# Causal attention with a routed feed-forward: maxima, exponentials, layer-norm steps and transposes in another order

## What is computed

```python
latent_kv = x @ w_kv_down;  kv = latent_kv @ w_kv_up        # keys and values, 16 heads of 64
q = (x @ w_q).reshape(Bx, Tx, N_HEAD, HEAD_SIZE)
att = jnp.einsum('bqhd,bkhd->bhqk', q, k) * scale
att = jax.nn.softmax(jnp.where(causal, att, -jnp.inf), axis=-1)
y = jnp.einsum('bhqk,bkhd->bqhd', att, v).reshape(Bx, Tx, HD) @ w_out
...
expert = jnp.argmax(feats @ centroids.T, axis=1)            # of eight
h = (xs - mu) * rsqrt(var + EPS) * g + b
y = xs + relu(h @ W1e.T + b1e) @ W2e.T + b2e                # the expert's own weights
out = alpha * y + (1.0 - alpha) * feats                     # alpha = sigmoid(feats . centroid)
```

## Time and profile before

| what | value |
|---|---|
| runs shown, median (lowest to highest) | 1460.65 us (1459.31 to 1461.14) |
| the profiled execution, its own time | 1459.58 us |
| its span, first to last instruction | 1457.7 us |
| mean granted TensorE clock, as a share of full speed | 0.977 |
| PE busy | 1343.0 us, 92% |
| DVE busy | 1234.4 us, 85% |
| ACT busy | 1083.2 us, 74% |
| POOL busy | 809.8 us, 56% |

### The profile page before, as it was taken

One profiled execution on the slowest core, in us unless ns is written; L12 is line 12 of the kernel. 1 busy time (PEld: TensorE's weight loads), 2 busy tenths in 40 slices (PEclk: granted clock), 3 DMA queues, 4 the chain that ended last, 5 costly groups with the idle time before them and its releaser, 6 DMA issues.

```text
span 1457.7 us, 34718 instructions
## 1 busy us (share of the span) xinstructions
PE 1343.0 (92%) x9120; PEld 1210.6 (83%) x9120; DVE 1234.4 (85%) x4806; ACT 1083.2 (74%) x3186; POOL 809.8 (56%) x1216
## 2 busy tenths in 40 slices
PE   7999999999999999999999999999999999599993
PEld 6988898888888988888888888888888888488872
DVE  5899888888888888888888888888888887499994
ACT  5888787878787878788787878787878886366661
POOL 3445555555555555555555555555555554178886
PEclk9999999999999999999999999999999999699997
DMA  4000000000000000000000000000000000312120
GB/s 194 5 9 12 12 11 12 11 8 11 12 11 12 11 11 10 9 11 11 11 11 12 11 10 11 10 11 12 11 12 11 9 9 14 95 48 63 59 62 8
DMA packets 38793, 32.39 MB, mean 22 GB/s; under 512 B 4882, under 2 KB 35990, under 8 KB 38304
## 3 DMA queue, kind: packets, MB, share of 16 engines
q1 hardware_dynamic: 31968, 21.61, 4.9%
q0 software_dynamic: 4608, 8.67, 1.7%
q10 hardware_dynamic: 2112, 1.11, 0.3%
HBM read 20.35 MB, written 12.07 MB: 22 GB/s over the span
## 4 chain that ended last, share of the span: by engine, by line
DVE 46%; issue 22%; ACT 18%; POOL 6%; PE 5%; ACTq 1%; DMA 1%; DVEq 1%; POOLq 0%; SPq 0%
DVE nscore L851 15%; DVE p_lo L861 13%; ACT prob L722 10%; ACT t_hi L694 5%; DVE nmax L851 2%; POOL prob L1037 2%; DVE ff L367 2%; DVE hitr L891 2%; DVE wup_s L384 1%; DVE on L393 1%; POOL pay L1056 1%; DVE fn L793 1%; DVE gg L402 1%; DVE t_lo L838 1%; DVE rinv L832 1%
## 5 line engine op out<-in xcount | busy, mean ns | idle before, releaser
L1037 POOL TENSOR_TENSOR prob<-prob,rinv 128x256 f32<-128x256 f32 (+1 forms) x512 | 413.2, 828 | 507.8 <-DVE rinv L832 507.7
L722 ACT ACTIVATE prob<-nscore,nmax 128x128 f32<-128x128 f32 (+1 forms) x1024 | 458.7, 449 | 248.4 <-DVE nmax L851 248.4
L851 DVE CUSTOM_DVE_ANT_0 nscore<-psS,mask 128x128 f32<-128x128 f32 (+1 forms) x1024 | 319.9, 350 | 0.0
L861 DVE TENSOR_TENSOR p_lo<-psP,p_hi 128x768 fp32r<-128x768 f32 x256 | 243.7, 952 | 1.0 <-ACT p_hi L694 0.9
L838 DVE TENSOR_TENSOR t_lo<-psT,t_hi 128x512 fp32r<-128x512 f32 x256 | 175.9, 687 | 56.0 <-ACT t_hi L694 56.0
L607 PE MATMUL psP<-ident,prob 128*128 128x128 f32 x1536 | 216.4, 277 | 6.8 <-DVE p_lo L861 6.7
L694 ACT ACTIVATE p_hi<-psP 128x768 fp32r<-128x768 f32 x256 | 204.9, 800 | 1.6 <-PE psP L607 1.6
L579 PE MATMUL psS<-t_lo,xt_hi 128*128 128x256 f32 (+1 forms) x512 | 196.8, 384 | 0.0
L722 ACT ACTIVATION_READ_ACCUMULATOR prob<-nscore,nmax 128x1 f32 x1024 | 191.3, 187 | 0.0
L607 PEld LDWEIGHTS psP<-ident,prob 128*128 128x128 f32 x1536 | 167.2, 141 | 22.7 <-POOL prob L1037 8.8
L867 DVE TENSOR_TENSOR z_lo<-psZU,z_hi 128x512 fp32r<-128x512 f32 x256 | 175.7, 686 | 3.3 <-ACT z_hi L694 3.3
(11 more groups left out here) (167 smaller groups left out, 3246.0 us busy)
## 6 DMA issues: line engine op xcount, KB each, us to landing
fin<-routed_rows SPq DMA_DIRECT2D x40, 136.0 KB, 2.2
wx<-ffn_w SPq DMA_DIRECT2D x2, 2058.0 KB, 12.0
xin<-x SPq DMA_DIRECT2D x32, 128.0 KB, 2.1
xres<-x SPq DMA_DIRECT2D x32, 128.0 KB, 2.1
out<-res,fin POOLq DMA_INDIRECT x80, 2.3
routed_rows<-padr ACTq DMA_DIRECT2D x4, 272.0 KB, 4.3
routed_rows<-padr SPq DMA_DIRECT2D x4, 272.0 KB, 5.4
wup_s<-wup SPq DMA_DIRECT2D x1, 1024.0 KB, 4.9
```

The costliest lines, as they stand in the source:

```text
L722: last = nc.scalar.activation(prob[:, p1, h, a:z], nscore[:, h, a:z], ACT.Exp, bias=nmax[:, p1, h, q:q + 1], scale=-1.0, accum_out=rsum[:, ...
L851: last = v.tensor_tensor_reduce(nscore[:, h, a:z], psQ[q][:, h, :], mask[:, a:z], -1.0, -MASKED, ALU.add, ALU.min, nmax[:, p1, h, q:q + 1])
L861: v.tensor_tensor(p_lo[:, (s - 3) % 2], psP[:, :, 0:384], p_hi[:, (s - 3) % 2].bitcast(F32), ALU.subtract).then_inc(S["p_split"], 1)
L1037: last = g.tensor_tensor(pr, pr, rinv[:, p2, :, q:q + 1].broadcast_to([P, 2, z - a]), ALU.mult)
```

## The change

Four orders are changed; no instruction is added or removed but one or two that a register needs.

1. PE: once the first few slots are over, P stands behind S, ahead of Z (new function `turn_probs`).
2. ACT: `exps(1)` follows `exps(0)` at once, and `z_hi` comes behind both.
3. DVE: `score_max(1)` stands ahead of `p_lo`. What `misc` did at the top of slots 0 to 3 (`an`, `st3`, `fn`, `st1`, `xn`) is now `block_norms`, between `score_max(1)` and `p_lo`; the aggregation of `st3` and `st1` is `block_moments`, behind `p_lo`. `xt_lo` (r = 6) and `st2` (r = 7) stay at the top. The last step of the routing's argmax, `oh`, now has `score_max(1)` ahead of it.
4. POOL: the two steps that make the reciprocal deviation for `fn` stay in slot 1 with semaphores of their own; the four that make the second one move to slot 2.

```diff
+            def turn_probs(g0, s, live):
+                p3 = (s - 3) % 4
+                pe.wait_ge(S["norm_ready"], g0 + s - 2)
+                if live(4):
+                    pe.wait_ge(S["p_split"], g0 + s - 3)
+                for h in range(2):
+                    for k in range(3):
+                        last = nc.tensor.transpose(psP[:, h, k * P:(k + 1) * P],
+                                                   prob[:, p3, h, k * P:(k + 1) * P], ident[:])
+                last.then_inc(S["pt_ready"], 1)
...
-                if live(3):
...
+                if live(3) and setup_slot(s, live):
+                    turn_probs(g0, s, live)
...
                         scores(q, (s - 1) % 2, xb, 2 * (g0 + s - 2) + 1 + q if live(2) else None)
+                if live(3) and not setup_slot(s, live):
+                    turn_probs(g0, s, live)
...
                 if live(1):
                     exps(0)
+                    exps(1)
...
                     cp(z_hi[:, (s - 4) % 2], psZ[:]).then_inc(S["z_hi_done"], 1)
-                if live(1):
-                    exps(1)
...
                 route(b0, s, live_b, 3)
+                if live(1):
+                    score_max(1)
                 route(b0, s, live_b, 4)
+                block_norms(b0, s, live_b)
                 if live(3):
                     dve.wait_ge(S["p_hi_done"], g0 + s - 2)
                     v.tensor_tensor(p_lo[:, (s - 3) % 2], psP[:, :, 0:384], p_hi[:, (s - 3) % 2].bitcast(F32),
                                     ALU.subtract).then_inc(S["p_split"], 1)
-                if live(1):
-                    score_max(1)
+                block_moments(b0, s, live_b)
...
-                    dve.wait_ge(S["r3_steps"], 6 * n - 4)
+                    dve.wait_ge(S["rs3_done"], n)
```

More of the change, by code:

```diff
@@ L149, in block_kernel @@
             bias_done bias_added weights_ready
-            x_loaded xr_loaded st1_done mv1_done ve1_done rs1_done xn_ready xk_hi_done xn_tr xt_hi_done x_split xk_split
+            x_loaded xr_loaded ve3_done rs3_done st1_done mv1_done ve1_done rs1_done xn_ready xk_hi_done xn_tr xt_hi_done x_split xk_split
             t_ready t_hi_done t_split s_ready nmax_ready probs_ready rinv_ready norm_ready pt_ready p_hi_done p_split
@@ L917, in route, with block_moments @@
                         v.tensor_copy(dst[:, db, :], dstf[:]).then_inc(S["dest_ready"], 1)
-            def misc_stats(b0, s, live_b):
+            def block_moments(b0, s, live_b):
                 r, db = s % PAIRS, s // PAIRS
@@ L925, in misc_stats, with block_norms @@
                     aggregate(st1, mv1, S["st1_done"], S["mv1_done"], b0 + db + 2)
+            def misc_stats(b0, s, live_b):
+                r, db = s % PAIRS, s // PAIRS
                 if r == 7 and live_b(1):
                     aggregate(st2, mv2, S["st2_done"], S["mv2_done"], b0 + db)
-            def misc(g0, b0, s, live, live_b):
+            def block_norms(b0, s, live_b):
                 r, db = s % PAIRS, s // PAIRS
+                n = b0 + db - 1
                 if r == 0 and live_b(2):
-                    n = b0 + db - 1
                     dve.wait_ge(S["rs2_done"], n)
@@ L962, in misc @@
                     prep_norm((db + 1) % 2, b0 + db + 2, b0 + db + 1)
+            def misc(g0, b0, s, live, live_b):
+                r, db = s % PAIRS, s // PAIRS
+                if not live(0) and s == 9:
+                    dve.wait_ge(S["bias_done"], E // 2 + 1)
+                    b1v = wx[:, :, B1:W2]
+                    v.tensor_tensor(b1v, psT[:, 0, 0:E * FB].rearrange("p (e j) -> p e j", e=E), b1v,
+                                    ALU.add).then_inc(S["bias_added"], 1)
                 if r == 6 and live_b(-1):
@@ L1044, in slot @@
                 if r == 1 and live_b(2):
+                    inv_sqrt(pay[:, db, :, C_RSTD], ve3, mv3[:, :, 1], S["mv3_done"], S["ve3_done"], S["rs3_done"],
+                             b0 + db - 1)
+                if r == 2 and live_b(2):
                     n = b0 + db - 2
-                    k = [6 * n]
+                    k = [4 * n]
                     def link(ins):
@@ L1053, in slot @@
                     rs3 = pay[:, db, :, C_RSTD]
-                    pool.wait_ge(S["mv3_done"], n + 1)
-                    link(g.tensor_tensor(ve3[:], mv3[:, :, 1], eps_t[:], ALU.add))
-                    link(g.tensor_tensor(rs3, ve3[:], neg_half[:], ALU.pow))
+                    pool.wait_ge(S["rs3_done"], n + 1)
                     link(g.tensor_tensor(w3[:, 0, :], mv3[:, :, 1], rs3, ALU.mult))
```

## The result

| | before | changed |
|---|---|---|
| median (lowest to highest) | 1460.65 us (1458.67 to 1461.83) | 1466.42 us (1465.76 to 1468.2) |
| ratio to before | | 1.0045, 95% interval 1.003 to 1.006 |
| profiled execution, its own time | 1459.58 us | 1467.72 us |
| its span | 1457.7 us | 1464.9 us |
| mean granted clock | 0.977 | 0.981 |

The account below looks back on a forecast made before the run. The prediction took a gapless ring of ACT and DVE, 4.30 us a slot, as the bound; 31 blocks x 0.32 = 9.9 and 14 branches x 0.37 = 5.2 made +15.1 us, a median of 1475.8, range 1448 to 1490.

Parts of the forecast that it names:

- the block's term: Sum of a block's eight slot steps: 37.37 us against 37.05, so 0.32 more, 9.9 us over 31 blocks.
- the detour for `oh`: Step into slot 5: PE waits for the late `oh`, delaying T, S and P; 4.90 us against 4.64 without.
- The ring: ACT and DVE cycle through both exponentials, `z_hi`, `z_lo`, `rinv`, `t_lo` and the maxima: 4.28 us a slot.
- PE's detour for `fn`: Step into slot 3: PE waits to transpose the late `fn`, delaying T, S and P; 4.95 us against 4.39 without.
- the four small steps: Step into slot 5: four small DVE steps at 0.09 us each count in full, making 4.64 us.
- The small steps at the top: DVE steps between `z_lo` and `t_lo` count in full: into slot 4 5.20 us, into slot 6 4.58.
- The branch: Loop's branch: DVE's stall, with nothing hiding it, costs 2.33 us a turn against 1.96; 14 x 0.37 = 5.2 us.
- POOL: POOL's moved deviation steps and its multiplication of P: 0 us, as POOL is busy 56% and P waits less.
- PE in the ring everywhere: Rival: PE's two-slot path, 8.45 us against 8.56, binds every slot if hand-overs are dearer; 12.4 more, 1488 us; chance 0.18.
- No detour was hidden: Judges the rival that PE's detours stay hidden: the two slots take 4.39 and 4.64, total 1450 us; chance 0.20.

## Where the prediction held, and the step that failed

The direction and the mechanism held: a new ring of nearly the length forecast, with what stays at the top counted in full, and a dearer branch. The size did not: 5.8 us for 15.1. **The step that failed is the block's term**, +0.32 us a block, 31 x 0.32 = 9.9 us; measured is +0.14, which makes 3.9 over the loop's 28 blocks. Its largest wrong part is the detour for `oh`, and the reason is one for several parts: durations of small DVE steps were taken from the earlier trace rows as their price, where they were waits for POOL. The parts one by one:

**The ring** was right, in its path and nearly in its length: 4.19 for 4.28. `rinv` takes 0.09, not 0.14, `t_lo` 0.57, not 0.60. Three slots a block were 0.28 us too dear.

**PE's detour for `fn`**: 4.82 for 4.95. Without it 4.39 was forecast and 4.41 measured; that this fits is in part luck, since it was 4.28 + 0.11 and came as 4.19 + 0.22. PE stood 0.2 us ahead of the transposes, where 0.5 was forecast.

**The detour for `oh`**: forecast 4.90, measured 4.57, what the four small steps alone make. So 0.26 a block, 8 us in 31, was charged for a detour that does not show; the other 0.07 is the ring's. The chain counted `oh` with 0.61 us from the earlier trace rows. That was the lock; now POOL's steps have just ended when `oh` comes, and it takes 0.16. With that in its place the prediction's own chain gives 4.45, less than the 4.64 of the small steps, and no detour. PE waits 0.66 us for `oh` in the mean, and this stays hidden.

**The small steps at the top** erred for the same reason, the other way. Slot 4's `hitr` went into the sum with 0.74 us, `dst`, between the two sets of maxima of slot 5, with nothing. Neither is a price of the step: each is the rest of POOL's multiplication, whose start hangs on `rinv`. In the new order `hitr` comes 0.59 us behind POOL's start instead of 0.83, and so it stands longer; `dst` takes 0.56. Into 4 0.20 and into 6 0.32 too cheap. That 16 numbers a row took 0.81 us, and the reduction of the same beside them 0.16, was to be seen before.

**The block** came out 0.14 dearer, not 0.32: 0.26 lower than forecast in its new length, and 0.08 in its old one. The prediction took 37.05 from the turn of the loop, where the falls of the clock and stragglers at the branch are averaged in; `exps(0)` to `exps(0)` gives 36.97. Over 31 blocks this is 5.6 of the 8 us between the forecast and the spans; rare events give 3.4 more, and the branch takes 2.7 back. The small rest is that the loop has 28 blocks and 13 taken branches, not 31 and 14, and what lies outside it. A turn of the loop took 76.7 us, not 77.1.

**The branch**: 0.52 more where nothing disturbs it, 0.56 in the mean, for 0.37. Its mechanism held: `an` no longer lies under the stall. It is the larger half of the loss.

**POOL** at 0 was right as a sum and wrong as a reason: POOL delays nobody by being late, but it holds DVE.

**Rivals.** PE in the ring everywhere: its sign is there, ACT waits for P in 194 slots of 256, and not in two of eight as forecast; its price is not, since PE's path has the same length. No detour was hidden but that for `oh`. What the prediction missed altogether: 4 turns of the kernel before lose 0.45 us to a fall of the clock, and the changed order has none. In that kernel, PE and then its stretch:

```profile
468.09 1.43 PE L607 MATMUL psP<-ident,prob 128*128 128x128 f32 x6 [0.41 <-DVE p_lo L861]
...
469.00:471.00 2.00, 2.00 (x9) 1.81 (x8) 1.68 (x8) 1.93 (x6) 0.96 (x2) 0.50 0.22 66
```

## What to carry to other kernels

Before a step's duration goes into a sum, ask whether it fits its size; where a few numbers take as long as hundreds, look for what ends at the same moment on another engine, since that part will change with any new order, and an operand in PSUM may take it away altogether. Two kernels are compared best by the starts of one step that recurs once in a round: the steps of a round show each gain and loss apart, and a mean over the loop mixes them with rare events. Parts of a reordering are not a sum of their own: P behind S does nothing alone, and without it the rest is 27 us slower.

## What the runs showed of the hardware

- A VectorE step whose inputs and output all lie in SBUF (`hitr`, two inputs; the copy `dst`, one) stood until GpSimd's running multiplication of SBUF operands ended, to 0.04 us: 1.06 and 0.56 us instead of 0.16. With an input in PSUM it never did (longest 0.175 and 0.160). A reduction of one small SBUF operand did not stand either (`dstf`, 0.16 beside the same multiplication, in every block of the loop). Where `hitr` started within 0.02 us of GpSimd's second instruction it stood in 26 blocks of 28 and came through in two, and then GpSimd's took 1.08 us instead of 1.04.
- DVE stands 2.3 us at the loop's branch with a body of two blocks (29.9 us in 13) and 2.6 with one of four (15.4 in 6): the stall belongs to the branch, not to the amount of code. PE, whose rows show 510 matmuls and as many weight loads a turn, crosses it in 0.2 us; with twice that it stands 3.6. The Trainium skill, Runtime: NRT & Kernel Launch, section Instruction fetch mechanics, gives PE room for 2048 instructions and most others for 512, and has a branch to code outside the engine's window wait for a fetch. PE's two cases agree with it. VectorE's case does not follow from the room alone: its body of two blocks has 384 rows, fewer than 512, and it stands in all 13 turns.
- PE's granted clock fell to 0.50 behind the branch in some turns and not in others, after much the same idle times ahead of T and ahead of P. With P ahead of S these were 0.96 to 1.21 and 1.74 us, and 10 turns of 13 fell; with `an` behind, 0.95 to 1.21 and 1.10, and 7 fell; in the kernel before, 1.24 to 1.47 and 0.41, and 4 fell. In the changed kernel they were 1.08 to 1.44 and 0.64, with S between, and none fell.
